# Attention and feed-forward kernel: loads, one value tile and the end's copies in other places

## The reference, cut to what matters

```
x1 = x + quaternion_rotation(x)                       # a 256x256 matrix that is built on the chip
n1 = g1(cond) * x1 / rms(x1) + b1(cond)
q, k, v = n1 @ Wq.T, n1 @ Wk.T, n1 @ Wv.T             # 16 heads of 16 channels
p  = softmax(q @ k.T / 4)                             # per batch and head, 1024 x 1024
a  = x1 + (p @ v) @ Wo.T
n2 = g2(cond) * a / rms(a) + b2(cond)
out = x1 + a + (silu(n2 @ gate.T) * (n2 @ hid.T)) @ out_w.T
```

## Time and profile before

| | us |
|---|---|
| median of 3 runs | 567.77 |
| lowest and highest | 564.28, 568.79 |
| the profiled execution | 568.51 |
| its span in the trace | 566.7 |
| PE busy | 540.9 (95%) |
| DVE busy | 398.9 (70%) |
| ACT busy | 371.5 (66%) |
| POOL busy | 156.6 (28%) |

### The profile page before, as it was taken

How to read it: one execution, slowest core, us unless ns; L and a number is a source line. 1 busy time by engine, 2 the same in 40 slices (tenths; PEclk the granted TensorE clock), 3 DMA queues, 4 the chain that set the end, 5 groups by cost and what they waited for, 6 DMA issues and landing times.

```text
span 566.7 us, 10750 instructions
## 1 busy us (share of the span) xinstructions
PE 540.9 (95%) x4214; PEld 301.2 (53%) x4214; DVE 398.9 (70%) x449; ACT 371.5 (66%) x736; POOL 156.6 (28%) x163
## 2 busy tenths in 40 slices
PE   8998979999999989999999999997969999999997
PEld 7866743333333333333333333333448888888886
DVE  5866688999989979999999999955345442121211
ACT  3647537988888878898899898895742432222322
POOL 4315621231131220010100001304258654232232
PEclk9999988999999989999999999998999999999999
DMA  5367584115346434424414411011010001010001
GB/s 210 113 143 182 200 189 76 32 54 122 78 88 107 83 82 69 88 45 72 92 44 66 87 41 33 16 38 31 12 39 10 0 2 38 0 38 2 31 7 37
DMA packets 24866, 38.21 MB, mean 67 GB/s; under 512 B 9384, under 2 KB 12072, under 8 KB 24808
## 3 DMA queue, kind: packets, MB, share of 16 engines
q1 hardware_dynamic: 23520, 32.81, 25.6%
q10 hardware_dynamic: 1296, 4.72, 2.9%
HBM read 22.24 MB, written 15.20 MB: 66 GB/s over the span
## 4 chain that ended last, share of the span: by engine, by line
PE 85%; DMA 5%; DVE 4%; POOL 2%; ACT 2%; issue 1%; SPq 1%; ACTq 0%; DVEq 0%; POOLq 0%
PE psum L1180 28%; PE psum L1197 26%; PE psum L1294 24%; PE psum L1276 2%; DVE nmax L1002 2%; DMA scr_max<-nmax_t 2%; DMA cond_bc<-in_cond 1%; PE psum L1318 1%; ACT prob L861 1%; PE psum L1157 1%; DVE f_raw L983 1%; DMA q_st<-scr_max 1%; PE psum L1237 0%; POOL at_lo L673 0%; POOL x L628 0%
## 5 line engine op out<-in xcount | busy, mean ns | idle before, releaser
L1002 DVE TENSOR_REDUCE nmax<-psum 128x1 f32<-128x1024 f32 x256 | 310.2, 1220 | 26.9 <-PE psum L1197 26.4
L861 ACT ACTIVATE prob<-psum 128x512 f32<-128x512 f32 x512 | 276.7, 598 | 49.3 <-PE psum L1276 27.1
L1197 PE MATMUL psum<-k_st,q_st 48*128 48x512 f32 x512 | 180.6, 450 | 6.3 <-DVE nmax L1002 5.5
L1276 PE MATMUL psum<-q_st,k_st 50*128 50x512 f32 x512 | 181.6, 451 | 2.5 <-DMA q_st<-scr_max 2.5
L1294 PE MATMUL psum<-prob,v_sb 128*17 128x256 f32 (+1 forms) x1952 | 161.8, 404 | 6.1 <-DVE ot L1038 3.4
L1197 PEld LDWEIGHTS psum<-k_st,q_st 48*128 48x128 f32 x512 | 73.8, 186 | 109.7 <-DVE nmax L1002 77.8
L1294 PEld LDWEIGHTS psum<-prob,v_sb 128*17 128x17 f32 x1952 | 33.3, 95 | 92.7 <-ACT prob L861 76.8
L1276 PEld LDWEIGHTS psum<-q_st,k_st 50*128 50x128 f32 x512 | 74.5, 187 | 11.5 <-ACT prob L861 5.0
L1141 DVE TENSOR_TENSOR h_f<-psum,silu_g 128x512 f32<-128x512 f32 x32 | 22.1, 690 | 83.0 <-PE psum L1180 77.5
L895 ACT ACTIVATE silu_g<-psum 128x512 f32<-128x512 f32 x32 | 19.1, 597 | 81.7 <-PE psum L1180 81.7
L725 POOL TENSOR_TENSOR h_lo<-h_f,h_hi 128x512 fp32r<-128x512 f32 x32 | 41.4, 1293 | 66.9 <-ACT h_hi L878 66.9
(11 more groups left out here) (116 smaller groups left out, 541.5 us busy)
## 6 DMA issues: line engine op xcount, KB each, us to landing
scr_qk<-qk_parts SPq DMA_DIRECT2D x16, 512.0 KB, 2.9
q_st<-scr_qk SPq DMA_DIRECT2D x42, 128.0 KB, 4.5
k_st<-scr_qk SPq DMA_DIRECT2D x42, 128.0 KB, 5.0
scr_o<-ot SPq DMA_DIRECT2D x16, 256.0 KB
f_raw<-in_ft ACTq DMA_DIRECT2D x6, 512.0 KB, 5.7
attn<-scr_o SPq DMA_DIRECT2D x64, 32.0 KB, 1.8
sums<-scr_sum SPq DMA_DIRECT2D x64, 32.0 KB, 1.8
x_t<-in_xt SPq DMA_DIRECT2D x3, 512.0 KB, 3.2
```

Of the source, the lines that this page charges most:

```text
L861: nc.scalar.activation(prob[(GH * s + h) % PR][:, :], e_bank("S", s, h), ACT.Exp).then_inc(e_used, 1)
L1002: nc.vector.tensor_reduce(out=nmax[:, b, e, pair, t:t + 1], in_=slot, axis=AX.XY, op=ALU.max, negate=True).then_inc(max_used, 1)
L1197: return nc.tensor.matmul(max_slot(item)[:, half, :], q_st[g % SLOTS][rows, pair, lt * P:(lt + 1) * P], k_st[g % SLOTS][rows, pair, half * ...
L1276: nc.tensor.matmul(e_bank("S", s, i), k_st[g % SLOTS][rows, pair, kt * P:(kt + 1) * P], q_st[g % SLOTS][rows, pair, half * HALF:(half + 1) ...
```

## The change

Six edits, no arithmetic added or taken away.

1. ACT's loads of f_raw go from steps 8r + 4 to 8r + 7, and POOL's splits from 8r + 7 and 8r + 8 to 8r + 10 and 8r + 11.
2. SP's load of a later group's stack goes from behind turn_outputs to right behind load_max, one block later.
3. The last value tile, ("V", 3, 1), leaves the preparation and becomes a side item of step 0, in a bank of the scores. paired changes with it.
4. In early and tail, QK(0, 2) changes places with V(0, 1), SC 2 goes behind the first pair, DVE's copies of L0 3 go behind the second pair, and the first norm_coefficients goes behind the scaling of chunk 0.
5. In the wide part, WO 1 leaves the loop for fin, y_T 0 goes one step later, and DVE's copy of O_BANK moves from step 120 into WO(0, 1), ahead of the squares and the scaling.
6. fin is written in another order, with POOL's add (RES) as a step of its own.

```
+        LATE_TILE = ("V", NCH - 1, 1)
...
-        placed = {WIDE: [("WO", 0, 0)], WIDE + 1: [("WO", 0, 1)], WIDE + 5: [("y_T", 0, 0)], WIDE + 6: [("y_T", 0, 1)],
-                  WIDE + 7: [("WO", 1, 0)], WIDE + 8: [("WO", 1, 1)]}
+        placed = {0: [LATE_TILE], WIDE: [("WO", 0, 0)], WIDE + 1: [("WO", 0, 1)],
+                  WIDE + 6: [("y_T", 0, 0)], WIDE + 7: [("y_T", 0, 1)]}
...
-        fw_loads = {8 * r + 4: r for r in range(6)}
-        fw_steps = {8 * r + 7 + i: 2 * r + i for r in range(6) for i in range(2)}
+        fw_loads = {8 * r + 7: r for r in range(6)}
+        fw_steps = {8 * r + 10 + i: 2 * r + i for r in range(6) for i in range(2)}
...
-        early += [("V", 0, 1), ("QK", 1, 0), ("QK", 1, 1), ("SC", 2), ("QK", 0, 2)]
+        early += [("QK", 0, 2), ("QK", 1, 0), ("QK", 1, 1), ("V", 0, 1)]
...
             for n in range(1, NG * NHALF):
                 load_max(n)
+                if SLOTS <= (n + 3) // NHALF < NG:
+                    load_stack((n + 3) // NHALF, ((n + 1) % NHALF,))
                 if n >= 2:
                     spread_inverses(n - 2)
                 turn_outputs(n - 1)
-                if SLOTS <= n // NHALF + 2 < NG:
-                    load_stack(n // NHALF + 2, (n % NHALF,))
...
                 wait_e_used(dve, *item)
+                    if item[2] == 1:
+                        copy_o_bank_late(WIDE // LT)
...
-        fin = ([("DIV", NG * NHALF - 2), ("CUT", 2), ("INV", NG * NHALF - 1), ("F", 0), ("y_T", 1, 0), ("y_T", 1, 1), ("F", 1), ("WO", 2, 0), ("WO", 2, 1),
-                ("DIV", NG * NHALF - 1), ("F", 2), ("SC", 2), ("CUT", 3), ("F", 3), ("F", 4), ("y_T", 2, 0), ("y_T", 2, 1), ("F", 5), ("WO", 3, 0), ("WO", 3, 1), ("F", 6),
-                ("SC", 3), ("F", 7), ("F", 8), ("y_T", 3, 0), ("y_T", 3, 1)]
-               + [("F", n) for n in range(9, len(ffn_units) + OUT_LAG)])
+        fin = [("DIV", NG * NHALF - 2), ("F", 0), ("WO", 1, 0), ("WO", 1, 1), ("F", 1), ("SC", 1), ("F", 2), ("INV", NG * NHALF - 1),
+               ("y_T", 1, 0), ("y_T", 1, 1), ("CUT", 2), ("F", 3), ("RES", 1), ("F", 4), ("WO", 2, 0), ("WO", 2, 1),
+               ("DIV", NG * NHALF - 1), ("F", 5), ("SC", 2), ("F", 6), ("y_T", 2, 0), ("y_T", 2, 1), ("CUT", 3), ("F", 7),
+               ("RES", 2), ("F", 8), ("F", 9), ("WO", 3, 0), ("WO", 3, 1), ("F", 10), ("SC", 3), ("F", 11),
+               ("y_T", 3, 0), ("y_T", 3, 1), ("F", 12), ("RES", 3)]
+        fin += [("F", n) for n in range(13, len(ffn_units) + OUT_LAG)]
```

More of the change, by code:

```diff
@@ L239, in build @@
         early += [("SEL", w, pair, 0) for pair in range(PAIRS) for w in (1, 0)]
[L240 removed]
+        early += [("QK", 0, 2), ("QK", 1, 0), ("QK", 1, 1), ("V", 0, 1)]
         early += [("SEL", w, pair, 1) for pair in range(PAIRS) for w in (1, 0)]
[L242 to L243 removed]
+        tail = [("SC", 2), ("L0", 3), ("SC", 3), ("QK", 0, 3), ("xs_T", 2), ("V", 1, 0), ("V", 1, 1),
+                ("QK", 1, 2), ("QK", 1, 3), ("xs_T", 3)] + [tile for tile in qkv(2) + qkv(3) if tile != LATE_TILE]
         pending = [("pair", u, u + 1) for u in range(0, HU + LEAD, 2)]
@@ L714, in _ @@
                     inverse_root(1, step[1])
-                elif step[0] == "WO" and step[2] == 1:
+                elif step[0] == "RES":
                     c = step[1]
@@ L774, in part1, with copy_values @@
                                          ).then_inc(free_sem("QK", c, j), 1)
+            def copy_values(c, pair, src):
+                t = c * CT + 2 * pair
+                return nc.scalar.activation(v_sb[:, t:t + 2, :, 0:DH],
+                                            src.rearrange("p (t h d) -> p t h d", t=2, d=DH), ACT.Copy)
             def copy_maxima(n, src):
@@ L1048, in _ @@
                 what, rest = step[0], step[1:]
-                if what == "L0":
+                if what == "L0" and rest[0] < NCH - 1 or step == ("SC", NCH - 1):
                     c = rest[0]
@@ L1053, in _ @@
                     copy_tokens(c)
-                elif step == ("V", 0, 1):
+                elif step == ("QK", 0, 2):
                     norm_coefficients(1)
@@ L1103, in _ @@
                 if s >= WIDE:
-                    if s % LT == 0:
-                        copy_o_bank_late(s // LT - 1)
                     for item in side_items(s):
@@ L1114, in _ @@
                     continue
-                if what in ("CUT", "DIV"):
+                if what in ("CUT", "DIV", "RES"):
                     continue
@@ L1232, in do_pair, with value_product @@
                             last.then_inc(max_filled[unit(item[1])[1]], 1)
+            def value_product(dst, c, pair):
+                hi, lo = xn_hi[c % 2], xn_lo[c % 2]
+                for i in range(2):
+                    t = slice((2 * pair + i) * P, (2 * pair + i + 1) * P)
+                    last = split_product(dst[:, i * D:(i + 1) * D], [(hi[:, kt, t], lo[:, kt, t]) for kt in range(KT)],
+                                         [(w_hi[:, 2, kt, :], w_lo[:, 2, kt, :]) for kt in range(KT)])
+                return last
             def transpose_maxima(n, dst):
@@ L1259, in do_side @@
                     last = transpose_maxima(n, dst)
+                elif what == "V":
+                    last = value_product(dst, n, item[2])
                 elif what == "WO":
@@ L1412, in _ @@
                     c, pair = rest
+                    if (c, pair) == (1, 0):
+                        pe.wait_ge(o_copied, 2 * NG * NHALF)
                     pe.wait_ge(at_lo_ready, KT * (c + 1))
```

35 lines of the change are left out of this document (13 added, 22 removed).

## The result

| | us |
|---|---|
| before, median of 20 runs | 571.79 (564.28 to 579.5) |
| changed, median of 20 runs | 561.81 (557.97 to 576.04) |
| ratio of the two | 0.9874, 95% interval 0.9837 to 0.991 |
| profiled execution of the changed kernel, its span | 565.83, 564.0 |

The change takes off 1.26%, 7.2 us (5.1 to 9.3); on the forecast's base of 567.8 that is 560.6. The sign is as forecast, but the forecast was 11.9 us: 561.8 lies just inside the bounds of the terms (551.5 to 562), outside the 554 to 558 of the forecast itself and outside the 552 to 561 that was given most of the mass.

A forecast was written before the change was run, and what follows sets the result against it. PE, busy for 95% of the span, was taken as the bound, with gains only where it waits or runs slowly. Terms -5.7 - 2.3 - 3.9 = -11.9 on 567.8 gave 556 us; forecast 554 to 558, terms' bounds 551.5 to 562.

The forecast's parts named there:

- edits 1 and 2: In the loop, blocks 2 to 8: the moved loads remove the whole loss, -5.7 us, bounds 0 and -6.
- late pairs: In the preparation: taking the value tile out shortens DVE's intervals between late pairs, -0.5 us.
- clock at the loop's start: Step 0: the value tile keeps PE busy, the clock stays up and DVE's idle times mostly go, -1.8 us.
- wide part, net: Before fin: PE's 3.37 us wait goes, fin starts 6.6 us earlier, 2.9 of it only moved, -3.7 us net.
- fin: In fin: 6.1 us lost before against 5.9 after the new order, -0.2 us, bounds -3 and +3.
- I take one slow stretch of 1.5 us: In fin: PE's waits of 4.4 us in sum are followed by one low-clock stretch, 1.5 us.
- rival (b): In fin: POOL's in-order queue bounds, slow stretches follow both waits, a third comes at the additions; +3.5, 559.5 us, chance 0.14.
- nobody on the path waits for these: POOL's normalise is due at step 112 or in fin: In the loop: the inverses' write, spread and outputs' turn, later behind the stack's load, delay nothing on the path.
- Rival (e): In the loop: late-landing weight rounds make POOL's splits delay the maxima in five blocks; +28, 584 us, chance 0.03.
- late blocks behind a stack alone lose no period: In the loop: evidence that weight rounds matter, as blocks 4 and 6 with both loads take 5.6 us.
- Full clock in the first three steps: At the loop's start: predicted sign, with no idle DVE there; a clock fall at step 0 would show it wrong.
- Rival (a): At the loop's start: the clock falls all the same; +2.8, 559 us, chance 0.15.

The follow-up runs named there:

- loads_only: The kernel before with edits 1 and 2 alone: ratio to the kernel before 0.9922 (0.9866 to 0.9978), 4.5 us of 572.75.
- tile_in_preparation: The changed kernel with edit 3 taken back, the last value tile in the preparation again: ratio to the kernel before 0.9897 (0.9843 to 0.9951).

## Why the prediction was wrong

| step | forecast | by the runs |
|---|---|---|
| edits 1 and 2 | -5.7 | -4.5 (loads_only, -1.3 to -7.7); -5.65 in a profile without the new wait, +1.5 and +1.9 in two with it |
| late pairs | -0.5 | -0.5 |
| clock at the loop's start | -1.8 | about -1.3 with the pairs' 0.5 in it (tile_in_preparation), -1.2 without (17.6 and 18.8 above); neither is resolved |
| edit 4 | 0 | +0.5 |
| wide part, net | -3.7 | 33.35 - 26.80 - 2.9 = -3.65 |
| fin | -0.2 | 157.0 - 152.5 - 2.9 = +1.6 with two low stretches; +0.1 or +0.2 with one; -1.3 with none |
| sum | -11.9 | -4.5 - 1.3 + 0.5 - 2.0 = -7.3 (measured -7.2; the first two terms are uncertain by 3 us or more each, so the closeness is luck) |

The measured gain is 4.7 us short of the forecast. No single step makes that up; fin has 1.8 of it, and the clock at the loop's start and the loop's new wait may have about 1 us each, within their noise. The stated range was also narrower than its terms: their bounds added up (-6, -2.6, -1.5, -3.7, -3 and 0, +0.5, +1, -3.7, +3) make 551.0 to 568.6 us, not 551.5 to 562.

**The step that failed most clearly is fin's "I take one slow stretch of 1.5 us".** The waits were right in place and nearly in size: 0.56, 2.11 and 2.10 us, 4.8 for the forecast's 4.4. A stretch costs the 1.5 us that were forecast. The mis-sized term is their number: two in five of the eight profiles with this fin, one in two, none in one. The earlier fin lies 152.5 - (149.9 - 2.9) = 5.5 us above a fin that has one wait of 0.66 left, so at 6.2, the forecast's 6.1. The change's with two stretches is 4.8 + 3.0 = 7.8, 1.6 more and not 0.2 less. With one stretch the forecast would have been right; the fault is to have taken one low stretch as the price where each of two waits can bring one. That is the first half of rival (b); its third wait, at the additions, didn't come.

**The second is "nobody on the path waits for these: POOL's normalise is due at step 112 or in fin".** It is due when POOL comes to it. Whatever stands behind it in POOL's queue waits for its sums, and edit 1 had put 3.9 us of splits there, ahead of nmax_t. Rival (e) named the right victim and the wrong cause (the landing of the round that POOL splits), and priced it for five blocks; it is one block, the fifth, and those four blocks took 0 to 7.5 us too long by the profile. In the median it weighs far less than in those two profiles: how often it strikes was not counted, and the 1.2 us between -4.5 and -5.7 is inside loads_only's interval.

**Edits 1 and 2** were right in sum and wrong inside. Not half and half: by the profiles either takes the delay under the slack, or to within 0.5 us of it, so the second to be made is worth nothing that was measured. The row on which the forecast rested (5.6 us with both) could not tell, and "late blocks behind a stack alone lose no period" was in fact the sign of slack, as was block 3 with its 3.98 us. The verdict that was drawn from the Trainium skill against the weights' half (DMA: Bandwidth & Descriptors, Queues, rings and completion order), no gain by the weights' move, held beside the stack's move (559.60 and 559.25 us), and for another reason than the one given: the 16 KB do notice a round on the other queue, 3.6 us instead of 1.4. Made alone, the weights' move gives the loop's loss back too.

**The clock at the loop's start.** "Full clock in the first three steps" was wrong in five of six profiles of the same instructions. This is the sign of being wrong that the prediction named, and it came. Rival (a) had the event right and its price too firm: a fall costs from 1.4 to 7.2 us there (16.4 and 22.1 against 14.94), so one profile can't carry a term of 1.8 us. Rival (a) alone would have given 559 us, near the 560.6 measured, but not as the whole cause, since fin was off as well.

**The wide part** went as worked out (-3.65 for -3.7), y_T 0's new wait included (1.26 us for 0.9). The four scalings ahead of it again took 4.00 us beside POOL.

## What to carry to other kernels

An in-order queue passes its waits on: before something is moved behind a step that waits for a transfer, ask not who needs that step, but what stands behind it, here four splits and then the maxima. When two things collide, look for the slack first, in a period that is late and loses nothing; then one of them may be enough, and the second edit can bring a cost of its own, as here. An engine's work whose input is ready early (the split for chunk 2) belongs into its idle time ahead of the busy stretch, and a wait on TensorE is to be priced with the clock behind it, once for each wait and as a range. Where executions differ by more than a term, that term can't be read from one profile.
